# Moving the residual and the closing normalisation of a mixture-of-experts layer into its expert tiles

## What is computed

```python
x = x + L0_xattn(layernorm(x), ctx)
x = x + L0_ffn(layernorm(x))        # self attention, then experts
x = x + L1_xattn(layernorm(x), ctx)
x = x + L1_ffn(layernorm(x))

# inside L0_ffn, after the self attention:
x = _ln(src + attn, n1_g, n1_b)
logits = xr @ moe_gate_w + moe_gate_b
top_v, top_i = top_k(logits, 2)
wts = softmax(top_v)
chosen = max(top_i)                 # one expert per token
def expert(W1, B1, G, Bt, W2, B2, rsc):
    hh = xr @ W1 + B1
    hh = gelu(_ln(hh, G, Bt))
    return (hh @ W2 + B2) * rsc + xr
moe = sel * sum(wts)                # sel: the chosen expert's output
return _ln(x + moe, n2_g, n2_b)     # called z below, before the _ln
```

## Time and profile before

| | us |
|---|---|
| median of 3 runs | 1917.64 |
| lowest and highest | 1911.63, 1920.36 |
| the profiled execution, its own time | 1912.33 |
| its span in the profile | 1910.6 |

### The profile page before, as it was taken

How to read it: one execution, slowest core, us unless ns; L and a number is a source line. 1 busy time by engine, 2 the same in 40 slices (tenths; PEclk the granted TensorE clock), 3 DMA queues, 4 the chain that set the end, 5 groups by cost and what they waited for, 6 DMA issues and landing times. The chain is left out here.

```text
span 1910.6 us, 29155 instructions
## 1 busy us (share of the span) xinstructions
PE 1682.8 (88%) x10228; PEld 790.3 (41%) x10228; DVE 1235.0 (65%) x2122; ACT 973.8 (51%) x1811; POOL 579.6 (30%) x637
## 2 busy tenths in 40 slices
PE   7899799899999999999999794899548997629997
PEld 4566454222222222222222374576434664215555
DVE  7444459788888888888883286566494554682222
ACT  5323154588888888888888330344375332202221
POOL 5200163343221211122111235466566000113533
PEclk9999999899999999999999896899879999758999
DMA  5000069532222222322200622222320000531542
GB/s 149 1 2 1 20 200 325 184 71 41 40 40 41 40 40 51 58 51 41 40 1 2 229 71 92 56 66 68 105 58 1 1 2 1 181 112 43 143 115 33
DMA packets 112864, 134.70 MB, mean 71 GB/s; under 512 B 18673, under 2 KB 88689, under 8 KB 112465
## 3 DMA queue, kind: packets, MB, share of 16 engines
q1 hardware_dynamic: 102016, 114.33, 22.2%
q0 software_dynamic: 9552, 17.97, 3.9%
q10 hardware_dynamic: 1152, 0.54, 0.1%
HBM read 78.60 MB, written 54.06 MB: 69 GB/s over the span
## 5 line engine op out<-in xcount | busy, mean ns | idle before, releaser
L1096 DVE TENSOR_REDUCE sa_mhalf<-sa_a 128x2 f32<-128x1024 f32 x512 | 604.2, 1221 | 85.5 <-PE sa_a L1308 83.7
L1241 ACT ACTIVATE sa_e<-sa_b 128x512 f32<-128x512 f32 x683 | 383.5, 601 | 76.9 <-PE sa_b L1341 76.9
L1351 PE MATMUL sa_b2o<-sa_e,sa_v 128*17 128x512 f32 x2048 | 270.3, 600 | 0.0
L1241 ACT ACTIVATE sa_e<-sa_b2o 128x512 f32<-128x512 f32 x341 | 205.0, 601 | 41.5 <-PE sa_b2o L1341 41.5
L1341 PE MATMUL sa_b<-sa_q,sa_k 112*128 112x512 bf16 x468 | 163.7, 389 | 2.7 <-ACT sa_e L1241 2.7
L1044 POOL TENSOR_TENSOR sa_rden<-sa_o_rows,sa_minus_one 128x16 f32<-128x16 f32 x32 | 93.1, 2908 | 178.1 <-ACT sa_o_rows L1224 178.1
L255 DVE TENSOR_REDUCE xa_mx<-xa_rows 128x16 f32<-128x1024 f32 x64 | 78.3, 1223 | 92.1 <-PE xa_rows L626 91.7
L1308 PE MATMUL sa_a<-sa_k,sa_q 48*128 48x512 bf16 x704 | 113.2, 389 | 13.4 <-DVE sa_mhalf L1096 13.4
L1033 POOL CAST sa_negm<-sa_neg 16x128 bf16<-16x128 f32 x32 | 9.4, 293 | 349.7 <-issue 339.0
L500 ACT ACTIVATE xa_pT<-xa_cols 128x1024 f32<-128x1024 f32 x64 | 62.1, 1022 | 80.8 <-PE xa_cols L658 80.8
L1341 PEld LDWEIGHTS sa_b<-sa_q,sa_k 112*128 112x128 bf16 x468 | 40.7, 97 | 151.1 <-ACT sa_e L1241 130.1
(11 more groups left out here) (345 smaller groups left out, 2953.8 us busy)
## 6 DMA issues: line engine op xcount, KB each, us to landing
k_parts<-sa_parts SPq DMA_DIRECT2D x96, 128.0 KB, 2.2
tc_w<-in_L_ffn_W SPq DMA_DIRECT2D x24, 512.0 KB
sa_q<-q_parts SPq DMA_DIRECT2D x44, 192.0 KB, 5.5
sa_k<-k_parts SPq DMA_DIRECT2D x44, 192.0 KB, 5.8
q_parts<-sa_parts SPq DMA_DIRECT2D x16, 384.0 KB, 3.4
ex_xg<-expert_in SPq DMA_DIRECT2D x39, 132.0 KB
v_groups<-sp_vt SPq DMA_DIRECT2D x8, 544.0 KB, 4.7
sa_v<-v_groups SPq DMA_DIRECT2D x16, 272.0 KB, 7.5
```

The source lines that it names most:

```text
L1096: nc.vector.tensor_reduce(mhalf[a % 2][:, half, head:head + PAIRED + 1:PAIRED, t], aps[a_slot(use)][:], axis=X, op=ALU.max).then_inc(a_use ...
L1241: nc.scalar.activation(ex[(KT * n + kt) % (LAG + 1)][:, head], bps[use % 3], ACT.Exp, scale=SCALE).then_inc(b_used, 1)
L1351: last = nc.tensor.matmul(ops[32 * head:32 * head + VW], vs[s][:, kt, head], ex[(KT * n + kt) % (LAG + 1)][:, head], start=(kt == 0), stop ...
```

## The change

The routing works out the sum of the weights per chunk, as share0 + share1 from the Tanh of half the difference of the two largest logits, and writes it into the second of the extra columns of each row, so that it travels with the row. The expert tiles multiply the result by it, add the row itself (the residual), and do the whole closing normalisation: moments on VectorE, the inverse root in a second column of the root that GpSimd makes for the hidden values, `center` (subtract the mean, times `n2_g`) on VectorE, the scaling by the root on ScalarE. The scatter writes the finished rows, two bodies later than before (k-4). Row and result buffers are eight each. Statistics and moments of the hidden values move behind other work in VectorE's order. Since nothing reads `src_rows` after the scatters of the routing, its room takes the next layer's weights, context, biases and `n2_g`, which SP loads after the first eight row tiles. In the second cross attention everything of z is gone: it adds the rows that it loads to x.

```diff
@@ class Context: the tiles may lie in a given room
+        for name, width in widths:
+            part[name] = kit.sb(name, [P, width])[:] if room is None else room[:, first:first + width]
@@ cross_attention, sync
-                        if c == 1:
-                            sp.dma_start(n2g[:], n2_g.partition_broadcast(P)).then_inc(g_loaded, 16)
-                        if c == 4:
-                            context.issue(sp)
-                            context.issue_output(sp)
@@ cross_attention, vector (weighted_sum and make_shift are removed)
                 def add_experts(c):
                     xs = x_sb[:, CT * c:CT * (c + 1), :]
-                    dve.wait_ge(zg_ready, c + 1)
-                    nc.vector.tensor_tensor(xs, xs, z[c % 4], ALU.add).then_inc(x_done, 1)
+                    dve.wait_ge(y_loaded[c], 16)
+                    nc.vector.tensor_tensor(xs, xs, yg[c], ALU.add).then_inc(x_done, 1)
...
-                if combine:
-                    weighted_sum(0)
-                    weighted_sum(1)
+                if not masked:
                     for step in range(CHUNKS + 2):
                         if step < CHUNKS:
-                            make_shift(step)
-                        if step + 2 < CHUNKS:
-                            weighted_sum(step + 2)
+                            add_experts(step)
+                            moments(step)
                         if 1 <= step <= CHUNKS:
-                            add_experts(step - 1)
-                            moments(step - 1)
-                        if step >= 2:
-                            make_x_shift(step - 2)
+                            make_x_shift(step - 1)
+                        if step == 1:
+                            place_key_bias()
                         if step == 3:
-                            place_key_bias()
-                        if step == 5:
                             place_values()
@@ cross_attention, gpsimd (invert and scale are removed)
+                    for c in range(CHUNKS):
+                        make_rstd(c)
+                        pool.wait_ge(rstd_ready, c + 1)
                     make_shares()
                     make_spread()
@@ cross_attention, scalar (normalize_z is removed)
+                    for step in range(CHUNKS + 3):
+                        if step == 3:
                             act.wait_ge(kbias_made, 1)
+                        if 3 <= step < 5:
+                            act.wait_ge(k_psum, step - 2)
                             for h in range(HH):
+                                place_keys(step - 3, h)
                         if 2 <= step < CHUNKS + 2:
+                            evacuate_xnT(step - 2)
+                        if 1 <= step < CHUNKS + 1:
+                            normalize_rows(step - 1)
+                        if step >= 3:
                             for half in range(HALVES):
+                                evacuate_qT(step - 3, half)
@@ attention_out, gpsimd
+                def weigh(c):
+                    pool.wait_ge(tanh_ready, c + 1)
+                    par = c % 2
+                    nc.gpsimd.tensor_scalar(share0[:, par], delta[:, par], -0.5, 0.5, ALU.mult, ALU.add).then_inc(weighed, 1)
+                    pool.wait_ge(weighed, 3 * c + 1)
+                    nc.gpsimd.tensor_scalar(share1[:, par], delta[:, par], 0.5, 0.5, ALU.mult, ALU.add).then_inc(weighed, 1)
+                    pool.wait_ge(weighed, 3 * c + 2)
+                    nc.gpsimd.tensor_tensor(src_rows[:, CT * c:CT * (c + 1), D + 1], share0[:, par], share1[:, par],
+                                            ALU.add).then_inc(weighed, 1)
+                    pool.wait_ge(weighed, 3 * (c + 1))
-                steps((invert, 0), (scatter_second, -4), (scatter_first, -3))
+                steps((invert, 0), (scatter_second, -4), (weigh, -3), (scatter_first, -3))
@@ attention_out, scalar
+                def compare(c):
+                    act.wait_ge(delta_ready, c + 1)
+                    nc.scalar.activation(delta[:, c % 2], delta[:, c % 2], ACT.Tanh, scale=0.5).then_inc(tanh_ready, 1)
-                steps((first_half, 3), (biased_gate, 2), (evacuate_xrT, -1), (second_half, 3))
+                steps((first_half, 3), (biased_gate, 2), (evacuate_xrT, -1), (second_half, 3), (compare, -3))
                 fill_behind(act, range(1, E8, 2))
-                act.wait_ge(delta_ready, 1)
-                nc.scalar.activation(delta[:], delta[:], ACT.Exp).then_inc(exp_ready, 1)
@@ attention_out, vector: in route(c)
+                    dve.wait_ge(top_done, CT * (c + 1))
+                    if c >= 2:
+                        dve.wait_ge(weighed, 3 * (c - 1))
+                    nc.vector.tensor_tensor(delta[:, c % 2], top[:, CT * c:CT * (c + 1), 1], top[:, CT * c:CT * (c + 1), 0],
+                                            ALU.subtract).then_inc(delta_ready, 1)
@@ attention_out, vector: at the end
-                nc.vector.tensor_tensor(delta[:], top[:, :, 1], top[:, :, 0], ALU.subtract).then_inc(delta_ready, 1)
-                dve.wait_ge(exp_ready, 1)
-                link(nc.vector.tensor_scalar(total[:], delta[:], 1.0, None, ALU.add))
-                link(nc.vector.reciprocal(total[:], total[:]))
-                link(nc.vector.tensor_tensor(delta[:], delta[:], total[:], ALU.mult))
-                link(nc.vector.tensor_tensor(wsum[:], delta[:], total[:], ALU.add))
@@ expert_tiles
-    U, AHEAD, LOADED, KEPT = 4, 3, 6, len(y_stored)
+    U, AHEAD, LOADED, KEPT = 4, 3, 8, len(y_stored)
@@ expert_tiles, sync
                 for k in range(LOADED):
                     load(k)
+                prefetch(sp)
                 for k in range(LOADED, MT):
                     passed(sp, xb_ready, k - LOADED + 3, turnstile)
                     passed(sp, xT_psum, k - LOADED + 1, turnstile)
+                    passed(sp, z_ready, k - LOADED + 1, turnstile)
                     load(k)
@@ expert_tiles, scalar: after gelu(k, j)
+                def normalize_result(k):
+                    act.wait_ge(centered, k + 1)
+                    act.wait_ge(rstd_ready, k + 2 + AHEAD)
+                    nc.scalar.activation(xb[k % KEPT][:], xb[k % KEPT][:], ACT.Copy,
+                                         scale=rstd[:, turn_of_result(k), 1:2]).then_inc(zn_ready, 1)
+                    if k >= 3:
+                        normalize_result(k - 3)
@@ expert_tiles, vector
-                    passed(dve, stats_done, k + 1, turnstile)
-                    nc.vector.bn_aggr(mv[:, j % 2], stats[:, j % 2]).then_inc(ln_stats, 1)
+                def hidden_moments(k, j):
+                    dve.wait_ge(stats_done, k + 1)
+                    nc.vector.bn_aggr(mv[:, turn_of_hidden(k), 0], stats[:, j % 2]).then_inc(ln_stats, 1)
+                def add_source(k):
+                    row = xg[k % LOADED]
+                    dve.wait_ge(y_ready, k + 3)
+                    nc.vector.scalar_tensor_tensor(out=xb[k % KEPT][:], in0=xb[k % KEPT][:], scalar=row[:, D + 1:D + 2], in1=row[:, 0:D],
+                                                   op0=ALU.mult, op1=ALU.add).then_inc(z_ready, 1)
+                def center(k):
+                    dve.wait_ge(z_stats, k + 1)
+                    nc.vector.scalar_tensor_tensor(out=xb[k % KEPT][:], in0=xb[k % KEPT][:], scalar=mv[:, turn_of_result(k), 1, 0:1],
+                                                   in1=n2g, op0=ALU.subtract, op1=ALU.mult).then_inc(centered, 1)
                 def body(k, turn, j, ahead):
                     if k >= 1:
                         finish(k - 1, (j - 1) % U)
                     if k + AHEAD - 1 < MT:
                         apply_norm(k + AHEAD - 1, (j + AHEAD - 1) % U)
+                    if k >= 2:
+                        center(k - 2)
+                    if k >= 1:
+                        add_source(k - 1)
                     if ahead:
                         add_b1(k + AHEAD, (j + AHEAD) % U, expert(dve, k + AHEAD))
+                    if k >= 1:
+                        result_stats(k - 1)
+                    if ahead:
+                        hidden_stats(k + AHEAD, (j + AHEAD) % U)
+                    if k >= 1:
+                        result_moments(k - 1)
+                    if ahead:
+                        hidden_moments(k + AHEAD, (j + AHEAD) % U)
...
+                dve.wait_ge(g_loaded, 16)
                 turns(dve, body)
                 finish(MT - 1, (MT - 1) % U)
+                add_source(MT - 1)
+                result_stats(MT - 1)
+                center(MT - 2)
+                result_moments(MT - 1)
+                center(MT - 1)
@@ expert_tiles, gpsimd
+                def make_rstd(turn):
+                    at = turn % 4
+                    if turn + AHEAD < MT:
+                        pool.wait_ge(ln_stats, turn + AHEAD + 1)
+                    if turn >= 1:
+                        pool.wait_ge(z_stats, turn)
```

(17 more changed lines are left out.)

190 lines of the change are left out of this document (70 added, 120 removed).

## The result

The changed kernel took 1894.48 us (median of four runs, 1890.66 to 1895.73), the kernel before 1917.64. The ratio is 0.988, with a 95% interval of 0.9853 to 0.9907. So it is faster, by about 1%: more than the 0.5% that can be told from nothing, more than forecast (0.994), inside the range. The profiled execution took 1894.03, with a span of 1892.3 us: 18.3 less than before.

The account below looks back on a forecast made before the run. TensorE was taken to bound the expert loop, a VectorE-GpSimd-ScalarE chain the front. Routing +2.0, loop +8.5, stage end +7.4 and front -30 gave -12.1: 1900.2 us own, 1905.5 median; predicted 1905, range 1890 to 1926.

Parts of the forecast that it names:

- the forecast's own range: Whole kernel: 1897 to 1915 us, from expert bodies of 4.2 to 4.45 and a front 26 to 34 shorter; chance 0.50.
- the rival in which VectorE stays hidden: Expert loop: root's wait covered, dispatch gaps vanish, body stays at TensorE's 4.10; 1893 us own, 1898.5 median; chance 0.12.
- Loop body, 4.30: Expert loop: VectorE's added instructions make it the bound; 35 bodies of 4.30 instead of 4.06 us, +8.5.
- Root wait 1.17: Expert loop: from the moments' end to apply_norm, VectorE waits 1.17 us for GpSimd's root, finish lying inside it.
- the signs named ahead: Expert loop and other stages: what would show the forecast, such as hidden_moments 4.3 us apart and TensorE busy about 95%.
- Start of the stage: Expert stage's beginning: no term of its own; row loads, the wait for the vector and prefetch traffic costed at nothing.
- End of the stage, 16.9: Expert stage, from body 35's moments to the last scatter's end: 16.9 us instead of 9.5, +7.4.
- The port: Expert loop: rival that center or add_source meets GpSimd's b2 addition, up to 0.73 us per body; 1931 median; chance 0.15.
- Routing, +2.0: Stage before the experts: eight chunks, each about 0.25 us longer on VectorE; GpSimd's small operations fall in idle time.
- the four removed operations: Routing's end: taking these and the Exp away gives nothing, as SP's last fill of the pads came later.
- Front, 66.4 + 2: Second cross attention's front without z: ends at 66.4 us, plus 2 for bias additions; -30.4, taken as -30.
- Biases, 2: Second cross attention: GpSimd's bias additions now reach into the attention and hold VectorE up, 2 us.

Follow-up runs that it names:

- loop_bare: Changed kernel without the expert tiles' residual sum, its statistics, moments, centring and result normalisation; expert stage 181.0 us instead of 190.9, body 4.10.
- read_once: Changed kernel with one register read less per expert body, and finish and centring ahead of the next apply_norm; 1883.41 us, 0.9863 of the kernel before.
- vector_between: Changed kernel plus one unused broadcast vector load behind the second chunk load of the second cross attention's front; front 63.2 us.
- both_lag3: Changed kernel with one register read saved, VectorE reordered, keys placed before chunk 0, and scatters three tiles behind instead of four; 1878.02 us, 0.9838 of the kernel before.
- port_meet: Changed kernel with GpSimd's b2 addition moved behind the inverse root, beside centring and residual sum; body 4.67 us, expert stage 206.5.
- routing_bare: Changed kernel without the routing's new weights in its chunk loop (VectorE's subtraction, GpSimd's weighing and comparison); expert stage started at 1197.12 us instead of 1197.74.
- before_weights_first: Kernel before, with the next layer's context and weights issued behind the front's second chunk load instead of the fifth; front 105.3 us instead of 98.8.
- after_again: The changed kernel unaltered, timed once more; 1892.77 us, 0.9914 of the kernel before.
- weights_late: Changed kernel with the next layer's context and weights issued inside the second cross attention's front again; span 1902.0 us, front 12.6 longer.

## Why the prediction was right, and where it was off

The sign and the mechanism held: the loop got longer by being handed over from TensorE to VectorE, and the front paid for it twice over. The size was too small. The median was forecast as 1905.5 and was 1894.48. Of these 11.0 us, 4.8 are no part of the mechanism: the kernel before had its median 5.3 above its profiled execution, I carried this over, and in the changed kernel the two differ by 0.5. The own time was predicted as 1900.2 and was 1894.03. The 6.2 us split by its terms: front -6.2, expert stage -1.1, routing -0.6, what follows +1.6. The result lies below the forecast's own range (1897 to 1915), and by time alone it is nearest to the rival in which VectorE stays hidden (1898.5). The rows refuse that rival: the body is 4.19, and it is back at TensorE's 4.10 only where VectorE's new instructions are left out (loop_bare) or its waits are covered (read_once). What brought the time there was a front 36.2 shorter, outside the 26 to 34 of the forecast.

**Loop body, 4.30.** Measured 4.19. Root wait 1.17 against 1.11, the rest 3.12 against 3.08. The 35 bodies took 148.1 against 142.0: +6.1, predicted +8.5. The steady 4.19 makes 4.6 of it (35 by 4.19 is 146.7), and three bodies of 4.65 another 1.4. The mechanism named was half right. I put the 1.17 down to the root, with the register read inside it. Here they end together (root at 1292.91, finish at 1292.96), and in read_once, which takes both off the path, the loop is back at TensorE's pace. Calling VectorE the bound was right: at its own length of 3.80 in read_once the loop is TensorE's again. Of the signs named ahead, TensorE's share came out as 99% and not 95%, and its clock in the loop stayed full.

**Start of the stage.** Costed at nothing, it was +0.9 up to the first moments inside the loop (21.4 us against 20.6), as tile 1's product ran at half clock. In vector_between it ran at full clock; there this stretch took 20.2 and the stage 189.7 instead of 190.9.

**End of the stage, 16.9.** Measured 17.35. Body 36 took 3.4 for 3.1 (finish waited for TensorE's product, 1.00 instead of 0.66), and the others were as worked out: 2.6, 2.6, 2.6, root 1.1, scatters 5.0. loop_bare shows what the sum didn't: 3.0 of the 7.8 us are the scatters' longer lag, of which one tile, 1.25 us, could be taken back (both_lag3).

**The port.** The rival's mechanism is real. Its price was 0.73 per body and is 0.48 (port_meet, 15.6 us for the stage), and what was said against it, the scatter ahead of the addition, is what keeps it out. It was overlooked that the first bodies have no scatter. It was also misread that the 1.19 in the earlier trace rows was "alone". At that time GpSimd's scaling started together with the addition, and it was GpSimd that paid, 3.39 instead of the 2.36 of its row at 1391.14:

```profile
1399.57 3.39 POOL L436 TENSOR_TENSOR xa_pT<-xa_pT,xa_n2g 128x1024 f32<-128x1024 f32 x1
```

The value holds all the same, for the addition at 1420.19, with GpSimd idle, took 1.19 too. But the pair says more than was read from it: which of the two pays depends on which starts first.

**Routing, +2.0.** That +1.4 came near it is luck, for the step was false. GpSimd's three small operations, costed at nothing because GpSimd has idle time in each chunk, cost 3.3 at the end of the stage: that idle time isn't there for the last chunks (routing_bare). VectorE's subtractions, costed at 0.25 each, cost something between 0 and 1 us in all. This pair of profiles shows only +1.4 because its kernel before has both the slower chunks and the longer end of the two profiles with the old routing; against before_weights_first it would be +2.9 by the stage's start and +5.0 from the first `max`. The claim that the four removed operations give nothing is neither borne out nor refuted.

**Front, 66.4 + 2.** Measured 62.6. This is the term that was mis-sized, by 3.8 before the biases, and it was mis-sized before the first scores (37.4 for 41.7). Chunk 0 landed 1.6 us earlier than before; I had taken its landing over from the earlier trace rows as a given, though the loads around it changed. The transposes of chunk 0 ran at full clock, 1.0 less (granted clock 0.87 in the whole front, 0.76 before). That one isn't sure to come: in after_again, the same program, they took 1.94 and the front 63.1. The rest, 1.7, is the chain between: 0.5 of it up to the end of chunk 0's projection, 1.2 from there to the end of the first scores. From the end of the first scores on, 24.7 us were predicted to the end and 25.2 measured. The prediction gave the early weights only that keys and values leave the path, without a number. weights_late puts 12.6 to it: a third of the gain.

**Biases, 2.** They now reach into the attention, and cost nothing there that shows. All that follows took 439.4 and 436.1 in the two profiles in which it and its biases are as before, and 435.5 to 441.0 in the twelve changed ones, eleven of them under 438. The +1.6 of this pair is within that.
